# moe_1 computes each token's two experts alone, on pages of 128 sorted slots; fronts and backs in blocks of their own

## The reference

```python
x = x + tanh(g_xattn[0]) * L0_xattn(layernorm(x), ctx, mask)
x = x + tanh(g_ffn[0])   * L0_ffn(layernorm(x))          # fp4 fake-quantised linear
x = x + tanh(g_xattn[1]) * L1_xattn(layernorm(x), ctx, mask)
x = x + tanh(g_ffn[1])   * L1_ffn(layernorm(x))          # "moe_1": 8 experts, top 2
x = x + tanh(g_xattn[2]) * L2_xattn(ctx, layernorm(x))   # "attention_2"
x = x + tanh(g_ffn[2])   * L2_ffn(layernorm(x))          # attention_2f, then a small MoE
x = x + tanh(g_xattn[3]) * L3_xattn(layernorm(x), ctx)
x = x + tanh(g_ffn[3])   * L3_ffn(layernorm(x))          # "moe_3": 64 experts, top 6
```

```python
h = relu(t @ W1[e] + b1[e])                  # 512 wide
h = (h - mean(h)) * rsqrt(var(h) + eps) * g1[e] + be1[e]
y = relu(h @ W2[e] + b2[e])                  # 128 wide
y = (y - mean(y)) * rsqrt(var(y) + eps) * g2[e] + be2[e]
```

## Time and profile before

| | |
|---|---|
| median of three runs | 1941.82 us (1941.77 to 1942.73) |
| span of the profiled execution | 1939.3 us |
| TensorE busy | 1830.3 us (94%) |
| VectorE busy | 1260.8 us (65%) |
| ScalarE busy | 912.1 us (47%) |
| GpSimd busy | 820.5 us (42%) |

### The profile page before, as it was taken

The page is one execution under the profiler, slowest core; times in us unless marked ns, Lnnn a source line. Parts: engine busy times, 40 slices in busy tenths (PEclk is TensorE's granted clock), DMA queues, the critical chain, the costliest instruction groups (busy, mean ns, idle before and its releaser), DMA issues. The chain is left out here.

```text
span 1939.3 us, 32871 instructions
## 1 busy us (share of the span) xinstructions
PE 1830.3 (94%) x11255; PEld 1217.3 (63%) x11255; DVE 1260.8 (65%) x3405; ACT 912.1 (47%) x2166; POOL 820.5 (42%) x1079
## 2 busy tenths in 40 slices
PE   6799999999999999999999999999999999999999
PEld 5466477566756657655766657756675676656656
DVE  6478577565777667566587747747575775764655
ACT  3254366275532556446543536627552662652221
POOL 2246166473530246565351217647352664630000
PEclk9899999999999999999999999999999999999999
DMA  6200000002044100001024200000200000033452
GB/s 243 74 1 1 0 2 1 1 15 74 1 141 135 46 1 2 1 1 63 27 73 149 89 11 1 2 1 1 88 1 1 1 1 1 2 118 119 136 166 87
DMA packets 53397, 91.11 MB, mean 47 GB/s; under 512 B 10480, under 2 KB 15216, under 8 KB 52592
## 3 DMA queue, kind: packets, MB, share of 16 engines
q1 hardware_dynamic: 53232, 89.01, 14.2%
HBM read 85.30 MB, written 3.69 MB: 46 GB/s over the span
## 5 line engine op out<-in xcount | busy, mean ns | idle before, releaser
L1349 POOL TENSOR_TENSOR rows<-rows,rinv 128x512 f32<-128x512 f32 x192 | 194.2, 1039 | 146.3 <-DVE rinv L1594 146.3
L2259 ACT ACTIVATE region_b<-psum 128x512 f32<-128x512 f32 x132 | 78.8, 597 | 225.8 <-PE psum L2221 225.5
L1519 ACT ACTIVATE rows<-psum,nmax 128x512 f32<-128x512 f32 x192 | 130.0, 683 | 111.5 <-DVE nmax L1587 111.4
L2233 PEld LDWEIGHTS psum<-region_c,region_b 128*128 128x128 f32 x1024 | 132.5, 192 | 54.1 <-issue 48.4
L1700 POOL TENSOR_TENSOR rows<-rows,rinv 128x128 f32<-128x128 f32 (+2 forms) x192 | 127.1, 684 | 75.5 <-DVE rinv L1869 75.5
L1586 DVE TENSOR_REDUCE lg<-psum 128x2 f32<-128x1024 f32 x128 | 155.5, 1215 | 3.5
L2297 DVE TENSOR_TENSOR region_b<-region_b,psum 128x512 f32<-128x512 f32 x128 | 87.5, 684 | 98.6 <-ACT region_b L2259 96.6
L1598 DVE COPY turned<-psum 128x512 f32<-128x512 f32 x128 | 88.4, 691 | 94.7 <-PE psum L1412 94.4
L1864 DVE TENSOR_REDUCE nmax<-psum 128x1 f32<-128x128 f32 (+3 forms) x256 | 113.6, 486 | 40.8 <-PE psum L1746 39.8
L1209 PEld LDWEIGHTS psum<-region_a,region_b 128*128 128x128 f32 x1024 | 122.2, 192 | 19.0 <-issue 16.1
L2233 PE MATMUL psum<-region_c,region_b 128*128 128x128 f32 x1024 | 133.6, 275 | 0.3 <-DVE region_b L2305 0.3
(11 more groups left out here) (489 smaller groups left out, 4030.8 us busy)
## 6 DMA issues: line engine op xcount, KB each, us to landing
pt<-gates SPq DMA_DIRECT2D x128, 128.0 KB, 3.0
ysb<-gates SPq DMA_DIRECT2D x128, 128.0 KB, 3.0
region_a<-in_w SPq DMA_DIRECT2D x32, 256.0 KB, 4.5
region_a<-in_eg SPq DMA_DIRECT2D x32, 256.0 KB, 3.4
region_c<-in_weights SPq DMA_DIRECT2D x32, 256.0 KB, 4.4
region_a<-in_eu SPq DMA_DIRECT2D x32, 256.0 KB, 3.5
region_a<-w_centred SPq DMA_DIRECT2D x24, 258.0 KB, 4.1
weights<-in_weights SPq DMA_DIRECT2D x1, 3489.0 KB, 15.7
```

The lines of the kernel that those rows point to most:

```text
L1349: nc.gpsimd.tensor_tensor(row(u, j), row(u, j), rinv[:, 2 * u + j:2 * u + j + 1].broadcast_to([P, S]), ALU.mult).then_inc(s.pn, 1)
L1519: nc.scalar.activation(row(u, j), s_bank(u, j), ACT.Exp, bias=nmax[:, 2 * u + j:2 * u + j + 1], accum_out=sum_column(u // T, u % T, j)).th ...
L2233: mm = nc.tensor.matmul(bank(7)[:, P * t:P * (t + 1)], htb[:, i % 2, P * t:P * (t + 1)], wd, start=(i == 0 and t == 0), stop=(i == n_items ...
```

## The change

moe_1 is computed for two batches (1024 tokens, a "group") at a time, and only for the two experts that each token takes. `route_1` normalises the tokens, finds the two largest logits, and counts with products against a triangular matrix of ones the slot of every token-expert pair, so that each expert's pairs fill whole pages of 128 slots. 2048 pairs and at most eight part-filled pages make 24 pages a group, whatever the routing. GpSimd scatters the normalised tokens into the slots in HBM (16 indirect transfers a group). `pages_1` walks the 48 pages. Each engine that needs a page's expert reads its number from SBUF into a register (`value_load`) and addresses weights and biases by it. The page's 128 tokens are now the stationary operand, so one product of 512 columns makes the hidden rows; they are turned by four transposes for the second matrix. Four pages are a "quad" for the loads, stores and normalisation. The finished rows go to HBM; for each batch eight indirect transfers gather every token's two rows, and DVE weighs and adds them (`combine_1`).

The blocks are now: setup with fronts 0 and 1; fronts 2 and 3 with route of group 0; the pages with route of group 1, and the gathers of batches 0 and 1; for b = 0 to 3 attention_2(b) and attention_2f(b), the gathers of batches 2 and 3 inside attention_2(0), and backs 0 to 2 together in one block after attention_2f(2); then moe_3(0), moe_3(1), moe_3(2) with back 3, moe_3(3). Work that stood between the normalisation and its use ahead of attention_2(0) and (3) is now done in the block before, as it was for batches 1 and 2.

```diff
-        front_beside_setup(0)
-        moe_1_beside_front(0, 1)
-        for b in range(B):
-            attention_2(next_block(), b, 1 <= b < B - 1)
-            if b + 1 < B:
-                attention_2f_then_moe_1(b)
-                moe_1_beside_back(b + 1, b)
-            else:
-                attention_2f_then_moe_3(b, b - 1)
-                moe_3_beside_back(b - 1, b)
-                moe_3_alone(b)
-            if b + 2 < B:
-                moe_3_beside_front(b, b + 2)
+        fronts_beside_setup()
+        fronts_beside_route()
+        moe_1_pages()
+        for b in range(B):
+            k = next_block()
+            late = ()
+            if b == 0:
+                s_late = sems(k % 2, LATE_1, sems(k % 2, ATTENTION_2))
+                late = (combine_1(s_late, 2, found_b[2]), combine_1(s_late, 3, found_b[3]))
+            attention_2(k, b, late)
+            if b < 2:
+                attention_2f(next_block(), b, xs[b + 1], keys_of(b + 1), LN_EPS)
+            elif b == 2:
+                attention_2f(next_block(), b)
+                backs()
+            else:
+                attention_2f_then_moe_3(b, 0)
+        moe_3_block(0, first=True)
+        moe_3_block(1)
+        moe_3_block(2, b_back=3)
+        moe_3_block(3)
```

The pieces of `pages_1` that the prediction speaks of:

```diff
+            def owner(eng, table, k, scale):
+                return eng.value_load(table[0:1, k // PAGES, k % PAGES:k % PAGES + 1], min_val=0, max_val=(E8 - 1) * scale)
+                def up(k):
+                    if k >= 2:
+                        pe.wait_ge(s.hb, k - 1)
+                    of_expert[k] = owner(nc.tensor, owner_pe, k, EXPERT_1)
+                    nc.tensor.matmul(up_bank(k), page_t[:, q % 2, P * j:P * (j + 1)], region_a[:, bass.ds(of_expert[k], F1)],
+                                     start=True, stop=True).then_inc(s.up, 1)
+                for k in range(n_pages + 2):          # tensor
+                    if k < n_pages:
+                        up(k)
+                    if 1 <= k <= n_pages:
+                        turn_hidden(k - 1)
+                    if k % 4 == 1 and k // 4 + 1 < n_quads:
+                        turn_rows(k // 4 + 1)
+                    if k >= 2:
+                        down(k - 2)
+                for k in range(n_pages + 9):          # scalar
+                    if 1 <= k <= n_pages:
+                        copy_hidden(k - 1)
+                    if k < n_pages:
+                        relu_and_square(k)
+                    if k >= 7 and k % 4 == 3 and k // 4 - 1 < n_quads:
+                        relu_rows(k // 4 - 1)
+                for k in range(n_pages + 9):          # vector
+                    if k < n_pages:
+                        add_bias(k)
+                    q = k // 4 - 1
+                    if 0 <= q < n_quads:
+                        if k % 4 == 1:
+                            hidden_var(q)
+                        if k % 4 == 2:
+                            rows_bias(q)
+                        if k % 4 == 3:
+                            rows_stats(q)
+                    if 0 <= q - 1 < n_quads and k % 4 == 0:
+                        rows_centre(q - 1)
+                        rows_add(q - 1)
```

More of the change, by code:

```diff
@@ L71, in flamingo_kernel @@
         stored = ctx.enter_context(nc.semaphore("outputs_stored"))
+        scattered_1 = [ctx.enter_context(nc.semaphore(f"rows_scattered_{g}")) for g in range(2)]
+        found_1 = [ctx.enter_context(nc.semaphore(f"rows_found_{b}")) for b in range(B)]
         def sb(name, shape, dt=FP32):
@@ L235, in flamingo_kernel @@
[L235 to L240 removed]
+        small_f = sb("small_f", [P, FRONT_SMALL])
@@ L246, in flamingo_kernel @@
         latv = sb("latv", [P, T, 2 * LAT])
-        y1 = sb("y1", [P, T, D])
+        g2_at = at["g2"][0]
+        y1s = [sb("y1", [P, T, D])] + [part(weights, g2_at + 512 * n, [P, T, D]) for n in range(2)]
+        y1s.append(y1s[0])
         m8 = sb("m8", [P, T, 8])
@@ L607, in interleave, with first @@
             due = [next(side, None) for side in sides]
+            def first():
+                return min((d, n) for n, d in enumerate([*due, float("inf")]) if d is not None)
             for step in main:
-                for n, side in enumerate(sides):
-                    while due[n] is not None and due[n] <= step:
-                        due[n] = next(side, None)
+                while first()[0] <= step:
+                    n = first()[1]
+                    due[n] = next(sides[n], None)
             while any(d is not None for d in due):
@@ L1706, in loop @@
                             yield u
-                    interleave(loop(), [ahead.gpsimd(pool)])
+                    interleave(loop(), [side.gpsimd(pool) for side in ahead])
                 @block.tensor
@@ L1797, in loop @@
                             yield step
-                    interleave(loop(), [ahead.tensor(pe)])
+                    interleave(loop(), [side.tensor(pe) for side in ahead])
                     add_output(groups - 1).then_inc(s.y, 1)
@@ L1846, in loop @@
                             yield step
-                    interleave(loop(), [ahead.scalar(act)])
+                    interleave(loop(), [side.scalar(act) for side in ahead])
                 @block.vector
@@ L1890, in loop @@
                             yield step
-                    interleave(loop(), [ahead.vector(dve)])
+                    interleave(loop(), [side.vector(dve) for side in ahead])
                     dve.wait_ge(s.y, 1)
@@ L2413, in moe_3_beside_back @@
             s2 = sems(k % 2, BACK, s3)
+            last = b == B - 1
+            sides = [] if b_back is None else [back(s2, b_back, bank(6), bank(5), set_f, back_1)]
+            if not last:
+                sides.append(norm_ahead(s3, xs[b + 1], set_m, bank(4), copy_xnt, 32, 34))
             def first_loads(sp):
```

974 lines of the change are left out of this document (549 added, 425 removed).

## The result

The changed kernel takes **1968.9 us** (1966.9 to 1971.0, 4 runs) against 1942.3 (1941.8 to 1943.3, 4 runs) before: ratio **1.0134, 95% interval 1.0122 to 1.0147**, slower by 26.6 us where +13 was forecast. The sign and the range hold, the size is half. The profiled execution has a span of 1965.9 us. The kernel before took 1940 to 1944 us in some runs and 1947 to 1952 in others of one later set, which widens the intervals given further down.

What follows compares the result with a forecast made beforehand. TensorE bounds the kernel before (1830 of 1939 us). 1377.4 stays, plus pages 247, setup 111, fronts with route 112, backs 95, late combines 10: 1952.4, as median 1955 us; forecast 1925 to 1985, overall range 1875 to 2015.

Steps and rivals of the forecast that it cites:

- the drain's own terms: End of setup with two fronts: 8 x 0.95 + 4 x 3.78 us at half clock, taken as 20.
- term 3: Second block, two fronts with route 0: 8.4 us start, 44 first part, 9 second front, 8 route, 22 scores, 21 drain: 112.
- Term 1: The page block: VectorE's queue takes 16.4 us a quad, 197 for 48 pages; with fills, route and waits 247.
- Step 0: VectorE's queue in a quad: 0.5 of a load, bias 0.7, centre and add 2.75; 3.95 us.
- step 2: VectorE's queue in a quad: a load and bias, four loads in a row, four biases; 5.4 us at 0.8 a load.
- my own sign: Page block: the forecast is wrong if a page takes less than 3.8 us.
- the first rival: Pages, fronts and backs: loads hide and chains overlap, a quad takes 13.8 us, kernel 1899 us; chance 0.36.
- gathers 3: Page block: GpSimd's gathers ahead of a square root add 3 us.
- The last rival: Second block, pages, attention_2(0): indirect transfers block GpSimd at 3.0 us instead of 1.25, +35, kernel 1990 us; chance 0.07.
- Term 4: Block of three backs: head 16 us, 26 and 15 paced by TensorE, tail 38; 95 us.
- Some 5 are the loads of a first moe_3: moe_3(2) with back 3, 120.7 us before: some 5 are loads that move to moe_3(0), no change in total.
- The clock rival: Page block: the clock falls to half, a page takes 5.0 us, the block 240 + 40 = 280, kernel 1988; chance 0.15.

Runs made afterwards that it cites:

- the earlier trace: The profiled run of the kernel before the change: span 1939.3 us.
- the first trace: The profiled run of the changed kernel from its first set of runs: span 1965.9 us.

## Why the prediction was right in sign and half in size

**Right.** That uncovered fronts and backs eat the gain. That no engine fills the page block, and that VectorE is waited for, with the idle times where the walk put them (2.06 us before the statistics, 2.00 at the loads). The price of a page on TensorE was near: 2.55 us in the plain quads (40.9 for sixteen pages) for 2.35. Setup with two fronts took 107 for 111, in which the drain's own terms add to 22.7 and not 20; the second front costs 23 us there (83.9 with one) and 24.6 in the second block, so most of its chain is hidden in both. attention_2(1) took 149.5. I had TensorE near 50% busy in the pages; it was 61.

**Right by luck.** TensorE's work fell by 139 us for the 140 of the experts, but I had the keeping-warm products on top, and they alone are 65. The late combines cost 10 us from product to product (160.2 for 150.1 without them) for 10, but 6 of my 10 were gathers ahead of GpSimd's scores. With the adds cut and all 16 gathers left, attention_2(0) took 151.7: the gathers cost under 2 and the adds the rest.

**The step that failed: term 3, "8 for route".** It priced the route by VectorE's instructions alone. VectorE was not full (73 of 126 us), and what the route added stood elsewhere too: 8 us in two waits at the head of in-order queues, behind which both fronts wait, and 9 us of products on TensorE, which was full at half clock just there and for which the sum had nothing. It cost 24 of the 53 us that it takes alone. With that the block would have been forecast at 128. A second part of the term was off and hidden by a third: the first product came 13.2 us into the block, not 8.4 (SyncE clears for 4.6 and then issues ten transfers), and the fronts' chain from there took 88 us, not 96.

**Term 1, two errors that cancelled.** The walk of a quad gave 16.4 us and it took 14.0: -29 over twelve quads. Step 0 took 2.7 for 3.95, step 2 3.9 to 4.2 for 5.4, the others came within 0.4. A load with its register instructions is 0.61 and not 0.8 (0.30 and 0.31, where I had 0.65 and 0.15), and the load of step 0 is hidden. The Trainium skill, DMA: Bandwidth & Descriptors, Latency and other measured facts, has a floor of about 600 ns for a `tensor_load`; the records here last 0.30 us, so it is no floor for these loads from SBUF. By my own sign, a page under 3.8 us, I was wrong: a plain page took 3.5. The quad is that of the first rival (13.8), at which that forecast a faster kernel. But everything around the quads, 50 in the sum, took 69: 7 before the first quad, 25 in quads that ran longer than 14.0 or, while the block fills, shorter, 22 more than a plain quad from the last quad's start to the last product, and 15 behind that. Of the long ones, the three beside the route cost 12 us more (I had 17). The one behind the scatters cost 10 and the one at combine 0's gathers 12, and my "gathers 3" was the part that counted work and not waits.

**The last rival** named this blocking, but not where it came. A transfer takes 0.94 to 1.24 us and 0.30 to the next, near the 1.25 that I had, not 3.0. In the second block the scatters cost under 2 us, in attention_2(0) the gathers under 2. Only in the pages did spreading give much, 17, and not because a transfer is dear: they stood in a run ahead of what other engines waited for.

**Term 4** gave 95 for three backs, 103.4 were measured. One alone took 68 and two more 18 each; which of head, middle and tail was short was not separated. The granted clock there was 0.82, so part of TensorE's 76.5 us (60 in the sum) is slow products; how much of the 8 us they cost was not tested.

**"Some 5 are the loads of a first moe_3"** was a misreading: moe_3(0), now the first, takes 95.3, and moe_3(2) with back 3 kept 122.3. The excess over moe_3 alone is the back's own TensorE time, 114.6 - 90.2 = 24.4 us in the earlier trace rows, the reading that I had made correctly for the front one sentence earlier.

**The clock rival** (1988) had every page at half clock. The plain quads ran at 1.00 with TensorE busy 41 of 56 us, and the page block as a whole at 0.83: 0.70 in the first two quads and 0.71 in the one behind the scatters. What that cost the pages was not tested. The two front blocks ran at 0.86 and 0.63, and the term for two fronts from rows at half clock was on the high side.

In attention_2(0) of the first trace the two idles of 2.6 and 2.9 us were each followed by a fall (0.91 and 0.86 in a stretch of 20 us), and the rest of the block had a mean of 0.96, where the cut adds give 1.00. Two other traces with the same two idles show a fall behind one of them only. The Trainium skill, TensorE: Matmul & The Clock Gate, A second HAM failure mode, says that short idles between groups of matmuls can make the clock alternate; the traces agree in part there, and in the plain quads, with idles in every page, they do not.

## What to carry to other kernels

Price a side chain on every engine that it touches, at the clock of that stretch, and add its waits: on in-order queues each wait of one chain holds the others. Here the route cost 24 us, 8 of the first 20 in waits and 9 on TensorE, where VectorE's work for it is 12. Beside a dense engine a chain's waits are hidden and its work on that engine is not: a back beside moe_3 cost 26 us, of which 21 to 24 are its own products. Where indirect transfers, register loads or adds must be interleaved, put them one or two per step, as early as their data allows, and read what later wait of the same queue they stand ahead of; with the inputs ahead of the clears, that turned 1.013 into 0.987, with no work taken away. When a forecast adds several terms, check each block against its own term afterwards, because a good total can be a sum of errors.

## What the runs showed of the hardware

- A register load from SBUF takes 0.30 us and its register instructions as long again, 0.61 us from load to load in a row. In these quads a load costs a mean of at most 0.4 us on VectorE's path: 39 us for 48 pages, of which placing them ahead of the waits recovered 14.
- Every accumulating ScalarE operation of the pages (L1297, L1300, 128x512) is two records: 0.63 us and an accumulator read of 0.19, 17.9 us for the reads over the page block.
- The same program took 1968.9, 1983.2 and 1978.6 us in three sets of runs, with the kernel before at 1942.3, 1942.2 and 1942.6. The standstill at the head of attention_2(0) is 7.6 us of it and lower clocks behind it some 5 more (0.92 for 0.96). It came with 16 indirect gathers in a row on GpSimd, in some sets only, and not with the chip: one chip had a set with it and one without. A change that adds such a run should be measured in more than one set.
